# The first batch's prologue of an adaLN attention and expert kernel: earlier loads, its own order of work, and extra matmuls on zeros

## The reference, cut to what matters

```python
# x: (8, 256, 256); 16 query heads, 4 key/value heads, head size 128; 8 experts
mod = (silu(c) @ wmod).reshape(8, 6, 1, 256)
sa, ca, ga, sb, cb, gb = (mod[:, j] for j in range(6))
ga = (2 * (ga >= 0) - 1) * maximum(abs(ga), 0.25)      # gb likewise
h = layernorm(x) * (1 + ca) + sa
q, k, v = h @ wq, h @ wk, h @ wv
q, k = rope(q), rope(k)
q = q / (norm(q) + 1e-6) * query_scale                 # k likewise
scores = tanh(q @ k.T / sqrt(128) / 50) * 50, masked to |i - j| <= 128
x = x + ga * ((softmax(scores) @ v) @ wo)
h = layernorm(x) * (1 + cb) + sb
x = x + gb * experts(h)                                # 8 gated experts, a router's weights
```

## Time and profile before

| | us |
|---|---|
| three runs | 886.4, 887.82, 1050.84 |
| median | 887.82 |
| the profiled execution | 888.83 |
| its span, first to last instruction | 887.1 |
| scores of slot 0 begin (in the span) | 51.47 |
| scores of slot 4 begin | 86.40 |

### The profile page before, as it was taken

The page is one execution under the profiler, slowest core; times in us unless marked ns, Lnnn a source line. Parts: engine busy times, 40 slices in busy tenths (PEclk is TensorE's granted clock), DMA queues, the critical chain, the costliest instruction groups (busy, mean ns, idle before and its releaser), DMA issues.

```text
span 887.1 us, 14076 instructions
## 1 busy us (share of the span) xinstructions
PE 820.9 (93%) x5056; PEld 726.2 (82%) x5056; DVE 558.4 (63%) x1117; ACT 389.9 (44%) x587; POOL 352.4 (40%) x473
## 2 busy tenths in 40 slices
PE   5678999999999999999999988695999999999996
PEld 4457998989988989989989977584788888888885
DVE  3768668577577586686685653638555655645657
ACT  3355556555555555555555442332232332332321
POOL 1677668577567586576686642100000000000000
PEclk9789999999999999999999999568899999999998
DMA  5520200000000000000000000310101101100001
GB/s 193 202 72 1 72 2 1 1 1 1 1 1 1 1 1 1 1 2 1 1 1 1 1 1 1 85 35 1 37 1 36 37 1 35 35 0 1 1 24 71
DMA packets 7615, 21.41 MB, mean 24 GB/s; under 512 B 1401, under 2 KB 3833, under 8 KB 7425
## 3 DMA queue, kind: packets, MB, share of 16 engines
q1 hardware_dynamic: 6544, 19.98, 6.8%
q10 hardware_dynamic: 1008, 0.61, 0.2%
HBM read 18.47 MB, written 2.11 MB: 23 GB/s over the span
## 4 chain that ended last, share of the span: by engine, by line
PE 83%; DVE 11%; issue 2%; ACT 1%; POOL 1%; DMA 1%; POOLq 0%; DVEq 0%; ACTq 0%
PE ps_o L455 13%; PE ps_proj L356 5%; PE ps_proj L357 4%; PE ps_proj L358 4%; PE ps_turn L401 3%; PE ps_g L356 3%; PE ps_g L357 3%; PE ps_g L358 3%; PE ps_u L357 3%; PE ps_u L356 3%; PE ps_u L358 3%; PE ps_d L356 3%; PE ps_d L358 3%; PE ps_d L357 3%; PE ps_y L356 3%; PE ps_y L357 3%
## 5 line engine op out<-in xcount | busy, mean ns | idle before, releaser
L455 PE MATMUL ps_o<-vaug,probs 128*128 128x129 f32 x1024 | 136.6, 277 | 7.7 <-DVE o_rows L904 5.1
L455 PEld LDWEIGHTS ps_o<-vaug,probs 128*128 128x128 f32 x1024 | 129.1, 192 | 14.8 <-issue 8.6
L701 ACT ACTIVATE ps_s<-ps_s 128x1024 f32<-128x1024 f32 x64 | 64.5, 1008 | 131.1 <-PE ps_s L358 131.1
L1167 POOL TENSOR_TENSOR root<-ssq,powers 128x4 f32<-128x4 f32 x80 | 82.6, 1033 | 94.0 <-DVE ssq L872 93.5
L900 DVE RECIPROCAL rden<-ps_o 128x2 f32<-128x2 f32 x128 | 21.7, 170 | 153.5 <-PE ps_o L455 153.5
L1070 DVE TENSOR_TENSOR mid<-ps_u,silu 128x512 f32<-128x512 f32 x64 | 44.2, 691 | 111.5 <-PE ps_u L358 111.2
L791 ACT ACTIVATE silu<-ps_g 128x512 f32<-128x512 f32 x64 | 38.2, 598 | 154.5 <-PE ps_g L358 154.4
L1178 POOL TENSOR_TENSOR prod<-prod 128x512 f32<-128x512 f32 x80 | 103.1, 1289 | 0.0
L875 DVE TENSOR_TENSOR prod<-ps_proj,cs 128x1024 f32<-128x1024 f32 x80 | 97.2, 1215 | 0.0
L356 PE MATMUL ps_proj<-w_hi,h_hi 128*128 128x512 f32 x192 | 86.3, 449 | 11.5 <-DVE w_lo L855 11.2
L1183 POOL TENSOR_TENSOR rows<-prod,rnorm 128x512 f32<-128x512 f32 x80 | 88.2, 1103 | 16.2 <-POOL prod L1178 7.9
(11 more groups left out here) (147 smaller groups left out, 1985.2 us busy)
## 6 DMA issues: line engine op xcount, KB each, us to landing
raw_e<-in_we SPq DMA_DIRECT2D x8, 768.0 KB, 4.2
raw_e<-in_wqkv SPq DMA_DIRECT2D x6, 512.0 KB, 6.8
raw_e<-in_wo SPq DMA_DIRECT2D x4, 512.0 KB, 3.7
out<-acc SPq DMA_DIRECT2D x4, 512.0 KB, 2.6
x_all<-in_x SPq DMA_DIRECT2D x1, 1792.0 KB, 10.0
x_all<-in_wmod SPq DMA_DIRECT2D x1, 1024.0 KB, 5.8
gates_a<-gate_rows_dram SPq DMA_DIRECT2D x1, 1024.0 KB, 6.1
gates_b<-gate_rows_dram SPq DMA_DIRECT2D x1, 1024.0 KB, 7.3
```

Source lines behind the costliest of these rows:

```text
L455: mm = pe.matmul(ps_o[:, h * (D + 1):(h + 1) * (D + 1)], probs[:, s % 2, at:at + P], vaug[:, b % 2, k, i // 2, :], start=(h == 0 and k == ...
L701: act.activation(ps_s[:], ps_s[:], ACT.Tanh).then_inc(tanh_done, 1)
L1167: pool.tensor_tensor(root[:, n % 2, :], ssq[:, n % 2, :], powers[:, 0:4], ALU.pow).then_inc(root_ready, 1)
```

## The change

- Batch 0 gets a schedule of its own: `FIRST` is -3, two units in each of the slots -3 to 2 (`FIRST_PROJ`), and turns by `FIRST_TURN`. Slots from 3 on are as they were.
- The six blocks of wq, wk and wv land in a buffer of their own, `raw_p`, which lies over `wo_hi` and half of `wo_lo` and is free of any ring; SP issues them one behind the other at the start, with three wo blocks behind them into `raw_e`. The fourth wo block is issued after block 6 is split. ACT's splits of wo wait until all six blocks are split.
- Blocks 0 and 1 are split ahead of the first slot, block 0 ahead of the modulation; the others at the ends of slots -3, -2, -1, 0, 1, 3, 5 and 7.
- The tables have a semaphore each, and `ident` and `cs` are issued by SP behind blocks 0 and 1.
- The rest of x is loaded as soon as the gate rows have been multiplied. The gate rows go to `ps_y`, ACT copies them out, and DVE works out the gates after slot 4; the gates go to DRAM and back then.
- `keep_busy(n)` issues n matmuls 128x128x128 in float32 on a zeroed piece of `probs`, into the second half of `ps_s`: 8 at the start, 3 after the modulation columns, 8 after the turn of h, and 4 ahead of each of the slots -2, -1 and 0.

```diff
-FIRST, LAST = -5, ALL + 1
+FIRST, LAST = -3, ALL + 1
+FIRST_PROJ = {-3: (0, 1), -2: (2, 3), -1: (4, 5), 0: (6, 7), 1: (8, 9), 2: (10, 11)}
+FIRST_TURN = {-2: (0, 1), -1: (2, 3), 0: (4,), 1: (5,), 2: (6, 7), 3: (8, 9)}
-SLOT_SPLIT = {-5: [1], -4: [2], -3: [3], -2: [4], -1: [5], 0: [6], 1: [7], 2: [8], 3: [9]}
+SLOT_SPLIT = {-3: [2], -2: [3], -1: [4], 0: [5], 1: [6], 3: [7], 5: [8], 7: [9]}
...
-    return [(b + later, p) for later, p in SLOT_PROJ[i] if 0 <= b + later < B]
+    first = [(0, p) for p in FIRST_PROJ.get(s, ())]
+    return first + [(b + later, p) for later, p in SLOT_PROJ[i] if 0 < b + later < B]
...
         @block.sync
-            sp.dma_start(wmod_sb[:, :, 0:2 * E], a["wmod"][:, :, 0:2 * E]).then_inc(wmod_in, 16)
-            sp.wait_ge(wmod_in, 16)
-            for c, (kind, n) in enumerate(LOADS):
-                if c >= RAW_RING:
-                    sp.wait_ge(w_lo_done, c - RAW_RING + 1)
...
+            sp.dma_start(wmod_sb[:, :, 0:2 * E], a["wmod"][:, :, 0:2 * E]).then_inc(wmod_in[0], 16)
+            for c in range(2):
+                sp.dma_start(raw_w(c), a["wqkv"][:, LOADS[c][1]]).then_inc(raw_in[c], 16)
+            sp.dma_start(ident[:], a["ident"]).then_inc(ident_in, 16)
+            sp.dma_start(cs[:], a["cs"]).then_inc(cs_in, 16)
+            for c in range(2, CHUNKS):
+                sp.dma_start(raw_w(c), a["wqkv"][:, LOADS[c][1]]).then_inc(raw_in[c], 16)
                 if c == 3:
+                    sp.dma_start(wmod_sb[:, :, 2 * E:], a["wmod"][:, :, 2 * E:]).then_inc(wmod_in[1], 16)
+            for c in range(CHUNKS, CHUNKS + RAW_RING):
+                sp.dma_start(raw_w(c), a["wo"][:, LOADS[c][1]]).then_inc(raw_in[c], 16)
+            sp.wait_ge(mod_rows, 1)
+            sp.dma_start(x_all[:, TT:NT, :], a["x"][:, TT:NT, :]).then_inc(x_in[1], 16)
+            sp.wait_ge(w_lo_done, CHUNKS + 1)
+            sp.dma_start(raw_w(CHUNKS + RAW_RING), a["wo"][:, RAW_RING]).then_inc(raw_in[CHUNKS + RAW_RING], 16)
+            sp.wait_ge(gate_rows, 5)
+            sp.dma_start(gates_dram, gfin).then_inc(gates_out, 16)
...
         @block.tensor
+            def keep_busy(count):
+                for _ in range(count):
+                    pe.matmul(ps_s[:, 1, 0:P], probs[:, 0, 0:P], probs[:, 0, 0:P], start=True, stop=True, skip_group_check=True)
+            pe.wait_ge(zeroed, 1)
+            keep_busy(8)
             pe.wait_ge(silu_c, 1)
-            pe.wait_ge(wmod_in, 16)
+            pe.wait_ge(wmod_in[0], 16)
             modulation_columns(ps_s[:, 0, :], (0, 1))
+            keep_busy(3)
             turn_h(0)
+            keep_busy(8)
             slot(FIRST)
...
-            for s in range(FIRST + 1, 0):
-                slot(s)
-            pe.wait_ge(gate_rows, 1)
             pe.wait_ge(mod_ready, 2)
-            for s in range(0, LAST + 1):
+            for s in range(FIRST + 1, LAST + 1):
+                if s <= 0:
+                    keep_busy(4)
                 slot(s)
...
         @block.scalar
+            split_w(0)
             columns(0, ps_s[:, 0, :])
             act.wait_ge(mod_ready, 2)
             modulate(0)
             h_head(0)
-            split_w(0)
+            split_w(1)
             slot(FIRST)
             columns(1, ps_o[:])
+            act.wait_ge(mod_rows, 1)
+            act.activation(grow, ps_y[0:B, :], ACT.Copy).then_inc(gate_rows, 1)
...
         @block.vector
+            split_w(0)
             h_tail(0)
-            split_w(0)
-            pending = slot(FIRST, [])
...
-            for s in range(FIRST + 1, LAST + 1):
+            split_w(1)
+            pending = []
+            for s in range(FIRST, LAST + 1):
                 pending = slot(s, pending)
+                if s == 4:
+                    gate_values()
...
         @block.gpsimd
+            pool.memset(probs[:, 0, 0:P], 0.0).then_inc(zeroed, 1)
             zero = pool.to_reg(0.0)
-            pool.wait_ge(consts, 80)
+            pool.wait_ge(powers_in, 16)
```

More of the change, by code:

```diff
@@ L73, in units_of @@
     b, i = divmod(s, SLOTS)
-    return [(b + later, p) for later, p in SLOT_PROJ[i] if 0 <= b + later < B]
+    first = [(0, p) for p in FIRST_PROJ.get(s, ())]
+    return first + [(b + later, p) for later, p in SLOT_PROJ[i] if 0 < b + later < B]
 def turns_of(s):
     b, i = divmod(s, SLOTS)
-    return [(b + later, r) for later, r in SLOT_TURN[i] if 0 <= b + later < B]
+    first = [(0, r) for r in FIRST_TURN.get(s, ())]
+    return first + [(b + later, r) for later, r in SLOT_TURN[i] if 0 < b + later < B]
 def turns_h(s):
@@ L132, in build @@
         w_lo = sba("w_lo", [P, CHUNKS, KT, CHUNK], F32R)
+        landing = ExitStack()
+        raw_p = sb("raw_p", [P, CHUNKS, KT, CHUNK], F32, landing)
+        landing.close()
         wo_hi = sba("wo_hi", [P, H, E], F32R)
@@ L217, in build @@
         x_in = [sem("x_first"), sem("x_rest")]
-        raw_in = [sem(f"raw_in{n}") for n in range(RAW_RING)]
+        raw_in = [sem(f"raw_in{n}") for n in range(len(LOADS))]
         expert_in = [sem("expert_in0"), sem("expert_in1")]
-        consts = sem("consts")
-        wmod_in = sem("wmod_in")
+        wmod_in = [sem("wmod_first"), sem("wmod_rest")]
+        ident_in = sem("ident_in")
+        zeroed = sem("zeroed")
+        powers_in = sem("powers_in")
+        cs_in = sem("cs_in")
+        qks_in = sem("qks_in")
         low_in = sem("low_in")
@@ L451, in weighted @@
                     pe.wait_ge(v_ready, TT * b + TT)
+                if s == 0 and t == 0:
+                    pe.wait_ge(mod_ready, 4)
                 for h in range(2):
@@ L462, in out_proj @@
                 pe.wait_ge(o_split, s + 1)
-                if pair == 0 and b:
-                    pe.wait_ge(y_gated, b)
+                if pair == 0:
+                    pe.wait_ge(y_gated, b) if b else pe.wait_ge(gate_rows, 1)
                 if b == 0:
@@ L508, in _ @@
                 for k in range(KT):
-                    mm = pe.matmul(ps_s[0:B, 1, j * E:(j + 1) * E], scT[:, k, :],
+                    mm = pe.matmul(ps_y[0:B, j * E:(j + 1) * E], scT[:, k, :],
                                    wmod_sb[:, k, block_of * E:(block_of + 1) * E],
@@ L931, in aggregate, with gate_values @@
                     dve.bn_aggr(mv2[:, TT * b + t, :], stats2[:, t, :]).then_inc(x2_aggr, 1)
+            def gate_values():
+                dve.wait_ge(gate_rows, 1)
+                dve.scalar_tensor_tensor(gabs, grow, -1.0, grow, ALU.mult, ALU.max).then_inc(gate_rows, 1)
+                dve.tensor_scalar(gsgn, grow, 0.0, 2.0, ALU.is_ge, ALU.mult).then_inc(gate_rows, 1)
+                dve.wait_ge(gate_rows, 3)
+                dve.tensor_scalar(gsgn, gsgn, -1.0, None, ALU.add).then_inc(gate_rows, 1)
+                dve.wait_ge(gate_rows, 4)
+                dve.scalar_tensor_tensor(gfin, gabs, 0.25, gsgn, ALU.max, ALU.mult).then_inc(gate_rows, 1)
             def slot(s, pending):
```

48 lines of the change are left out of this document (17 added, 31 removed).

## The result

The changed kernel takes 872.3 us (median of its four runs) against 887.1 for the kernel before (also four): the ratio is 0.984, with an interval of 0.9815 to 0.9866. One run of each kernel, 1039 and 1051 us, was in a slower state of the chip; the two medians count them, the ratio doesn't, and the other three runs alone have medians of 872.15 (872.1 to 872.5) and 886.4 us (885.0 to 887.8). The forecast was 875.5 with a range of 868.5 to 883.0, and no change of 2%: the time lies inside. The gain is 14.8 us by the medians and 16.7 by the two profiled executions (888.83 and 872.15), since that of the kernel before lay 1.7 above its own median. What follows goes by the profiles, where a mark can be read to a tenth of a us. But each profile is of one execution, and executions of one kernel differ: 13 of the kernel before in one job took from 885.0 to 889.6 us.

A forecast was written before the change was run, and what follows sets the result against it. Bound by a start-up chain before slot 4's scores, with TensorE busy afterwards. 17.0 us won there, less 2.3 collisions, 2.0 clock and 0.4 later duties, gives 12.3: a median of 875.5 us, range 868.5 to 883.

The forecast's parts named there:

- The bound: TensorE is 93% busy, nearly always from slot 4; only the chain before slot 4's scores, at 86.40 us, can shrink.
- The first projection, 14.8 to 12.5: Start-up: block 0's split leaves the path, and a clock rising mid-stretch starts the first projection at 12.5 us, not 14.8.
- Units 0 and 1: First two units' projections: 1.4 us each at full clock, 2.6 at half; 3.4 taken for both.
- To the scores of slot 0: From unit 2 at 20.5 us, DVE's list sets the pace, with about 2 us waiting for `w_lo`; scores at 34.4.
- To the scores of slot 4: From slot 0's scores, steps of 5.0, 10.9, 10.4 and 8.7 us reach slot 4's at 69.4 instead of 86.40.
- The reserves: Held back from the gain before slot 4: 2.3 us for DVE and POOL collisions, 2.0 for TensorE's clock.
- Later duties: Four gate instructions on DVE after slot 4 and two splits in slots 5 and 7, mostly hidden: 0.4 us.
- The signs: Slot 4's scores at 70 to 77 us; wrong before 68, after 80, or if slots 5 to 7 grew over a us.
- Rival 3: Before slot 4, the `w_lo` wait becomes a wait on DVE's and POOL's lists: 883.5 us, chance 0.08.
- Rival 1: TensorE's clock stays low, at first or again in slots -1 to 1: gain 6.1, time 881.7 us, chance 0.20.
- Rival 2: Full clock from the modulation on, no collisions, no hole before slot 4: gain 18.9, time 868.9 us, chance 0.13.
- Rival 4: In slots -2 to 2, two units run DVE and POOL by turns and slots grow: 895.9 us, chance 0.03.

The follow-up runs named there:

- late loads: Changed kernel with block 0 issued after wmod's first part landed, blocks 3 to 5 only once block c-3 is split: 873.4 us, ratio 0.9835.
- gates one by one: Changed kernel with one of DVE's four gate instructions at the end of each of slots 4 to 7: 870.6 us, ratio 0.9813.
- two and two: Changed kernel with two of DVE's gate instructions after slot 4 and two after slot 6: 871.2 us, ratio 0.9815.
- the better kernel: Changed kernel, ident ahead of block 0, later blocks after wmod's first part, 12 start zeros, none before slot -2, gate instructions one per slot: 868.4 us.
- all edits together: Changed kernel, powers ahead of x, zeros 13, 3 and 11, none ahead of slot -2, two gate instructions after slot 4, two after slot 6: 872.9 us.

## Why the prediction was right, point by point

**The bound** was read rightly: all that was won lies before slot 4, and TensorE's steady slots kept their 6.84 us.

**The first projection, 14.8 to 12.5: this step failed.** It came at 14.62. The choice was for a clock that rises in the middle of the stretch and so hides the eight zeros after the turn. In the profiled execution it rose and fell again. Windows of the changed kernel (columns as in rows 2):

```profile
7.00:8.00 1.00, 1.00 (x10) 1.00 (x10) 0.10 (x2) 0.28 (x1) 0.00 (x0) 0.88 0.89 307
8.00:10.00 2.00, 1.40 (x6) 1.10 (x6) 0.38 (x2) 0.93 (x3) 0.90 (x2) 0.50 1.06 396
...
12.00:14.00 2.00, 2.00 (x12) 2.00 (x11) 0.60 (x1) 1.97 (x4) 0.00 (x0) 0.50 1.05 424
```

It was full when the modulation ran (16 records in 1.93 us from 5.99, half of the 3.55 in rows 6), fell at 7.8, TensorE having been idle from 4.66 to 5.99, and was low until 14.6. So the eight zeros took 3.5 us at 0.44 each, the price given for half clock, and ended at 14.6, half a us after h was ready at 14.09. The end at 14.7 that the text worked out for half clock is what came, but by another sum: modulation shorter, the turn later. Two terms in it were wrong. The first part of `wmod` landed after 5.0 us, not 0.8 sooner than 5.2. That is not the weight blocks' doing: with late loads, where neither tables nor blocks went beside it, it took 4.9, and in the kernel before with zeros, where the tables did, 4.9 as well; moving the tables was worth nothing. And nothing was reckoned for `powers`, whose delay is 1.5 us at the normalised rows. (`ident`, issued at 2.6 and landing after 6.9, would have held the turn till 9.5 as well.)

How the clock goes there is not fixed by the code. The two kernels with spread gates have the same code up to slot 4, but in their profiles the clock did not rise on the first zeros at all. With gates one by one:

```profile
6.11 3.56 PE L390 MATMUL ps_s<-scT,x_all 128*128 128x8 f32 x16 [1.27 <-DMA x_all<-in_wmod]
9.52 1.63 PE L529 MATMUL ps_s<-probs 128*128 128x128 f32 x6
10.94 1.06 PE L417 MATMUL ps_turn<-ident,xn 128*128 128x128 f32 x4
11.80 2.78 PE L529 MATMUL ps_s<-probs 128*128 128x128 f32 x16
14.57 0.50 PE L380 MATMUL ps_proj<-w_hi,h_hi 128*128 128x512 f32 x1
```

The modulation took 3.56 us, at half clock, the turn followed the zeros without a wait for late rows, and the clock rose at 13.5. That is nearly the prediction's sum at half clock, and the first projection came at 14.57 (14.32 with two and two), as in the other course. What decides between the two courses was not tried. So none of the small steps at the head can be ascribed to an edit from one profile, and the 7.0 us of the better kernel may be partly luck; its gain in time, which four runs show, is not.

**Units 0 and 1** were priced at 3.4 us, between the clocks; they took 2.8, 0.23 apart from the first on, since the zeros had brought the clock up as the last of them ended. Unit 2 came at 21.95, not 20.5: of the 2.1 us lost at the head 1.45 were left.

**To the scores of slot 0** the laid time was 13.9 us, and it took 13.98 (21.95 to 35.93). The wait for `w_lo` before unit 5 was forecast at 2 us and was 0.8: the split ran at 1.22, and POOL's rows for the turns, named "second in line", took over.

**To the scores of slot 4** 35.0 us were laid and 33.5 passed. From slot 0 to 1 5.19 (laid 5.0), then slots 1, 2 and 3 in 9.78, 9.85 and 8.68 (laid 10.9, 10.4 and 8.7). So the mark came at 69.43 where 69.4 was laid, which is partly luck: 1.5 us late at slot 0, 1.5 us better after it. Part of the reason for the better half is in the groups by line of the changed kernel up to 69.4 us:

```profile
L1221 POOL TENSOR_TENSOR rows<-prod,rnorm 128x512 f32<-128x512 f32 x10 | 11.4, 1141 | 2.9 <-issue 1.3 <-POOL prod L1216 1.1
L891 DVE TENSOR_TENSOR w_lo<-raw_p,w_hi 128x1024 fp32r<-128x1024 f32 x6 | 8.4, 1408 | 0.3 <-ACT w_hi L670 0.3
```

POOL's rows took 1.14 us in the mean and the splits 1.41, against 1.34 and 1.56 in rows 8; the split of block 5, laid at 1.6 in slot 1, took 1.19. The rest of slot 1's 1.1 us was not followed up.

**The reserves were the step most at fault for the size.** With them the forecast had the mark at 73.7, and it came at 69.43. 2.3 us were kept for more collisions of DVE and POOL; there were fewer, though POOL was busy 89% in one stretch. 2.0 us were kept for the clock; it did not fall once between the first projection and the end of stage A. Without zeros it did, for 3.4 us at slot 0's scores. Together 4.3 us not needed.

**Later duties** were put at 0.4 (0 to 2) and cost 1.8, all of it the block of four gate instructions: the mean idle share of DVE was taken for cover, where the question was how long DVE is idle in that one place. It was 1.5 us at the end of slot 4, for 3.7 us of instructions.

**The signs.** One that the prediction named as a sign of being wrong came: slots 5 to 7 grew by 1.8 us in all, over the one us it allowed. Slot 4's mark lay 0.6 before the 70 to 77 it gave, and after the 68 below which it would be wrong. The other signs came as told: DVE busy 34.8 and POOL 37.2 of 45.4 us from 24 us to slot 4, both over 70%, slot 0 at 35.93, and the waits for `w_lo` at 0.8, below the 2 or 3.

**After slot 5** nothing was forecast, and 1.4 us more were won in the rest, where the code is the same. From the start of slot 63's scores to the end the kernel before takes 887.1 - 539.76 = 347.3 us and the changed one 870.3 - 524.41 = 345.9. The first stretch of it in the kernel before:

```profile
539.76:600.00 60.24, 48.45 (x238) 43.23 (x237) 27.54 (x50) 21.26 (x34) 7.89 (x7) 0.72 0.18 45
```

and in the changed one, then in the one with late loads:

```profile
524.41:584.65 60.24, 46.74 (x235) 41.52 (x234) 27.21 (x50) 21.26 (x34) 7.89 (x7) 0.75 0.17 45
```

```profile
524.72:584.96 60.24, 48.46 (x232) 43.10 (x231) 26.83 (x49) 21.25 (x34) 7.89 (x7) 0.69 0.17 45
```

The same work gets a clock of 0.72, 0.75 or 0.69 there, and the rest of the kernel takes 347.3, 345.9 or 349.9 us. That it is the clock fits these rows; what sets it at that place was not tried. It need not be the kernel: the profiled execution with late loads (876.46 us) was 3 us over the other three of the same kernel (872.8 to 873.6), and all other profiles have 345.5 to 347.4 us there. So the 1.4 us may be those of two executions. In the profile 12.3 + 4.3 (reserves) - 1.4 (gates) + 1.4 (the rest) = 16.6, measured 16.7.

**The rivals.** Rival 3, that the waits only change their name, had 4.3 us of gain, and 17.0 came at the mark. Rival 1, the low clock, did happen at the head, but not in slots -1 to 1. Rival 2 would have had 19.3 us at the mark, and its full clock at the head did not come; but from the first projection on the reserves for collisions and holes were not needed, as it said. Rival 4's mean slot of 10.6 us or more never came: it was (69.43 - 14.62) / 7 = 7.8.

## What to carry to other kernels

When a start-up chain is slow, look first at where the preparatory work stands in each engine's list. Here the waits for splits, 11.2 us, went with their place in the lists and the order of work, while the early landing of the blocks was worth 0.3 us at most and held up a small table by 2.5. Duties moved out of the start need a place as long as they are: a mean idle share hides nothing, and four short instructions one per slot were free where the same four in a block cost 1.8 us. Zeros that keep TensorE's clock up are worth trying only together with the view of the granted clock, since in single profiles they gained 4.9, lost 1.5 and gained 2.0 us in three orders of the same work, and by the runs never more than about 1.5. A profile is one execution: before a difference of a us or two is explained, it has to be seen in a second profile or in the runs.

## What was not expected of the hardware

- A load of 8 KB took 4.3 or 6.8 us to land by what the other queue was carrying, and put ahead of the 256 KB of x it delayed x from 4.8 to 6.2 us.
- In the changed kernel the clock rose at 4.4 us on zero matmuls alone, fell at 7.8, behind a hole of 1.3 us and a row of modulation matmuls only 8 columns wide, and came back at 14.6 behind a full run of zeros. With all edits together, where the start zeros reached the modulation without a hole, it stayed full through the same modulation.
- The same zeros at the head, in code that is the same up to slot 4, left the clock low until 13.5 us in two other profiles. The first projection and slot 4's scores came within 0.3 us of the same times all the same.
- In the same code after slot 63 the mean granted clock of the first 60 us was 0.69 to 0.75 in three profiles and the rest took 345.9 to 349.9 us; the longest was an execution 3 us over the others of its own kernel. So small edits are told by marks inside the trace, and those by more than one profile.
